# Pair 2's first round by seven products, with the weights' differences made in pairs 0 and 1

## The reference

```
att   = softmax(gelu(gelu(cond @ W0 + b0) @ W1 + b1) @ W2 + b2)      # 64 x 8
agg_w = einsum('bk,koi->boi', att, weight)                           # 64 matrices of 64 x 64
c     = einsum('boi,bih->boh', agg_w, x) + (att @ bias_k)[:, :, None]
out   = c @ W.T + b                                                  # W is 1024 x 1024
lora  = c @ A[:r].T @ B[:, :r].T        # r of (8, 16, 32, 64) by the largest gate score of c
x     = x + out + lora
```

## Time and profile before

| | us |
|---|---|
| median of 3 runs | 445.14 (444.48 to 445.39) |
| the profiled execution | 446.35 |
| its span | 444.8 |
| outside the span | 1.55 |
| PE busy | 438.8 (99% of the span) |
| DVE busy | 277.7 (62%) |
| ACT busy | 125.6 (28%) |
| POOL busy | 21.9 (5%) |

### The profile page before, as it was taken

One profiled execution on the slowest core, in us unless ns is written; L12 is line 12 of the kernel. 1 busy time (PEld: TensorE's weight loads), 2 busy tenths in 40 slices (PEclk: granted clock), 3 DMA queues, 4 the chain that ended last, 5 costly groups with the idle time before them and its releaser, 6 DMA issues.

```text
span 444.8 us, 10164 instructions
## 1 busy us (share of the span) xinstructions
PE 438.8 (99%) x3639; PEld 409.9 (92%) x3639; DVE 277.7 (62%) x695; ACT 125.6 (28%) x262; POOL 21.9 (5%) x46
## 2 busy tenths in 40 slices
PE   8999999999999999999999999999999999999996
PEld 6979999998999999999999999999999999999995
DVE  5959959695573747557374755837475483747533
ACT  5654543532230402223040222314022221302210
POOL 3014000010000000000000000000000000000000
PEclk9999999999999999999999999999999999999999
DMA  7985662607144170714408061340806135070303
GB/s 242 325 237 176 161 212 62 229 1 243 48 153 140 30 264 0 238 51 151 138 14 275 0 235 55 142 147 9 280 0 225 64 140 149 12 273 7 96 1 94
DMA packets 24363, 59.17 MB, mean 133 GB/s; under 512 B 7198, under 2 KB 9298, under 8 KB 24276
## 3 DMA queue, kind: packets, MB, share of 16 engines
q1 hardware_dynamic: 24020, 58.71, 41.1%
q10 hardware_dynamic: 320, 0.14, 0.1%
HBM read 40.69 MB, written 18.15 MB: 132 GB/s over the span
## 4 chain that ended last, share of the span: by engine, by line
PE 97%; DMA 1%; SPq 0%; issue 0%; DVEq 0%; ACT 0%; DVE 0%
PE p_p L1054 79%; PE p_o L1076 8%; PE p_o L1113 4%; PE p_o L1114 4%; DMA w_raw<-in_w 1%; PE p_p L1157 1%; PE p_p L1102 1%; PE p_p L1209 0%; DVEq L87 0%; ACT wh L567 0%; SPq L381 0%; SPq L379 0%; SPq L377 0%; SPq L376 0%; PE p_p L1165 0%
## 5 line engine op out<-in xcount | busy, mean ns | idle before, releaser
L1054 PE MATMUL p_p<-wh,xh 128*128 128x274 f32 (+1 forms) x880 | 258.9, 294 | 0.4 <-ACT wh L567 0.4
L1054 PE MATMUL p_p<-wh,xl 128*128 128x274 f32 (+1 forms) x880 | 254.5, 289 | 0.0
L1054 PE MATMUL p_p<-wl,xh 128*128 128x272 f32 (+1 forms) x864 | 250.1, 290 | 0.4 <-issue 0.4
L1054 PEld LDWEIGHTS p_p<-wh,xh 128*128 128x128 f32 x880 | 166.5, 189 | 7.5 <-issue 6.6
L1054 PEld LDWEIGHTS p_p<-wh,xl 128*128 128x128 f32 x880 | 166.5, 189 | 0.1
L1054 PEld LDWEIGHTS p_p<-wl,xh 128*128 128x128 f32 x864 | 163.0, 189 | 0.6 <-issue 0.6
L778 DVE TENSOR_TENSOR xl<-raw,xh 128x512 fp32r<-128x512 f32 x45 | 31.1, 691 | 49.4 <-ACT xh L598 49.0
L612 ACT ACTIVATE z<-p_p 128x272 f32<-128x272 f32 (+1 forms) x44 | 17.6, 399 | 116.7 <-PE p_p L1054 116.7
L800 DVE TENSOR_TENSOR xl<-s_raw,xh 128x512 fp32r<-128x512 f32 x60 | 40.2, 687 | 16.3 <-ACT xh L604 15.8
L831 DVE TENSOR_TENSOR xin<-p_o,xin 128x274 f32<-128x274 f32 (+2 forms) x128 | 46.3, 414 | 2.1 <-PE p_o L1114 1.3
L824 DVE TENSOR_TENSOR z<-p_p,su 128x274 f32<-128x274 f32 (+1 forms) x56 | 24.7, 441 | 31.8 <-PE p_p L1054 31.4
(11 more groups left out here) (123 smaller groups left out, 288.1 us busy)
## 6 DMA issues: line engine op xcount, KB each, us to landing
xin<-in_x SPq DMA_DIRECT2D x32, 512.0 KB, 4.2
raw<-in_xt SPq DMA_DIRECT2D x30, 512.0 KB, 4.1
out<-xin SPq DMA_DIRECT2D x15, 512.0 KB, 3.2
out<-xin SPq DMA_DIRECT2D x30, 256.0 KB, 3.5
w_raw<-in_w SPq DMA_DIRECT2D x8, 274.0 KB, 7.6
w_raw<-in_w SPq DMA_DIRECT2D x8, 272.0 KB, 6.6
g_aggw<-aggw_all SPq DMA_DIRECT2D x8, 128.0 KB, 2.5
aggw<-g_aggw SPq DMA_DIRECT2D x15, 64.0 KB, 3.3
```

Source lines behind the costliest of these rows:

```text
L1054: last = nc.tensor.matmul(o[:, 0:W[r]], a, m, start=start and p == 0, stop=stop and p == 2, skip_group_check=True)
```

## The change

Round 0 of pair 2 becomes sevenfold: `TERMWISE` goes from 2 to 1. Pair 2 then has no A21 parts and no termwise evictions, but a snapshot, sums of products and S1 to S4 in round 0. The differences of round 0's weights move:

- the four `t_sum(0, ...)` (8 DVE instructions) go from pair 2 to pair 0: R11 and R12 ahead of `route(0, 0)`, R22 and R21 behind the low part of `bt`. For this DVE's `column_sums` moves behind all of `w_lo`, and round 1's `t_sum` are spread: R12 behind pair 0's residuals, R22 behind A12's low part, R21 into pair 1;
- `t_hi(0, ...)` on ACT go to pair 1: R22 ahead of the eviction of Z21, R11 behind it, R12 and R21 at the pair's end;
- `t_lo(0, ...)` on DVE: R22 and R11 in pair 1, R12 and R21 in pair 2's round 0.

```
-T_LOWS = ((R22, R12, R21, R11), (R22, R11, R12, R21))
-TERMWISE = 2
+T_LOWS = (R22, R11, R12, R21)
+TERMWISE = 1
...
@@ ACT, step(i, j)
-                    if not two:
-                        snapshot(i, j, 0)
+                    snapshot(i, j, 0)
...
-                if two:
+                if one:
                     t_hi(0, R22)
-                    t_hi(0, R12)
-                if early(i, j, 0):
                     z_evict(i, j, 0, Z21)
-
-                if two:
-                    t_hi(0, R21)
+                    t_hi(0, R11)
                 snapshot(i, j, 1)
                 if not last:
                     a_hi(i, j + 1, A11)
-                if two:
-                    t_hi(0, R11)
                 z_evict(i, j, 1, Z11)
                 if not last:
                     a_hi(i, j + 1, A12)
                 u_transposed(i, j)
+                if one:
+                    t_hi(0, R12)
+                    t_hi(0, R21)
...
@@ DVE, pair 0
-            w_lo(12)
+            for m in range(12, 16):
+                w_lo(m)
             column_sums()
-            for m in range(13, 16):
-                w_lo(m)
+            t_sum(0, R11, R12, R11)
+            t_sum(0, R12, R22, R12)
             route(0, 0)
             ...
+            dve.wait_ge(s_tsum[0], 4)
+            t_sum(0, R22, R22, R11)
+            dve.wait_ge(s_tsum[0], 6)
+            t_sum(0, R21, R21, R22)
             dve.wait_ge(s_wl, 16)
             t_sum(1, R11, R12, R11)
-            t_sum(1, R12, R22, R12)
-            dve.wait_ge(s_tsum[1], 4)
-            t_sum(1, R22, R22, R11)
             a_lo(0, 1, A11)
             for n in (Z11, Z22, Z12, Z21):
                 residual(0, 0, 0, n)
+            t_sum(1, R12, R22, R12)
             a_lo(0, 1, A12)
-            dve.wait_ge(s_tsum[1], 6)
-            t_sum(1, R21, R21, R22)
+            dve.wait_ge(s_tsum[1], 4)
+            t_sum(1, R22, R22, R11)
...
@@ DVE, step(i, j)
                 if one:
+                    dve.wait_ge(s_tsum[1], 6)
+                    t_sum(1, R21, R21, R22)
...
                     s_lo(i, j, S4)
-                elif two:
-                    (four t_sum(0, ...), s_lo S3 and S4 between them)
                     t_lo(0, R22)
-                    t_lo(0, R12)
                 else:
+                    if two:
+                        t_lo(0, R12)
                     add(i, j, 0, SU2)
                     s_lo(i, j, S3)
+                    if two:
+                        t_lo(0, R21)
                     s_lo(i, j, S4)
...
                 add(i, j, 1, SU2)
-                if two:
-                    t_lo(0, R21)
+                if one:
                     t_lo(0, R11)
```

More of the change, by code:

```diff
@@ L686, in step @@
                 one = is_pair(i, j, 1)
-                two = is_pair(i, j, TERMWISE)
                 if one:
@@ L765, in t_lo @@
                     ks = slice(2 * h, 2 * h + 2)
-                    dve.wait_ge(s_th[r], 2 * T_LOWS[r].index(n) + h + 1)
+                    dve.wait_ge(s_th[r], 2 * T_LOWS.index(n) + h + 1)
                     nc.vector.tensor_tensor(wl[r][:, T_OF[n], ks, :], w_raw[r][:, n, ks, :],
@@ L970, in step @@
                 one = is_pair(i, j, 1)
-                two = is_pair(i, j, TERMWISE)
+                two = is_pair(i, j, TERMWISE + 1)
                 if not one:
@@ L1290, in low_difference @@
                     if first:
-                        pe.wait_ge(s_tl[r], 2 * T_LOWS[r].index(n) + 2)
+                        pe.wait_ge(s_tl[r], 2 * T_LOWS.index(n) + 2)
                 def end(done):
```

## The result

The changed kernel takes 443.29 us in the median of 22 runs. The kernel before, run beside it, takes 445.37 us (22 runs). The ratio is 0.9956, with a 95% interval of 0.994 to 0.9971: 2.0 us less, 1.3 to 2.7. Forecast were 443.0 us and 2.18 us less. One of the 22 runs took 1187.17 us at a full granted clock, for which nothing here gives a cause: it is left out of the ratio, and without it the median is 443.19 us. The kernel was run twice more beside the experiments and had ratios of 0.9967 (0.9948 to 0.9986) and 0.9932 (0.9906 to 0.9957).

A forecast was written before the change was run, and what follows sets the result against it. PE was taken to bound the kernel, busy 438.8 of 444.8 us. Fewer matmuls (1.52) and a closed gap (0.66) sum to 2.18 us off the 445.14 median, giving 443.0 us, range 442.4 to 443.9.

The forecast's parts named there:

- both terms: On PE: 1.52 us from 12 fewer matmuls and 0.66 us from a closed gap; chance of both 0.66.
- 12 matmuls fewer, 1.52 us: Pair 2's round 0 on PE falls from 96 to 84 matmuls, with its step from 13.20 to 11.68 us.
- The gap, 0.66 us, from a late S21: PE's gap ahead of pair 3's mix, blamed on DVE's late S21 sum in pair 2, goes: 0.66 us.
- The moved sums hide in two holes of pair 0: DVE's four added sums fill idle ahead of column sums and route; route on time, A12's slack 0.45 us, cost 0.
- ACT's added roundings don't reach PE: In pair 1 two roundings delay Z21's eviction by 0.62 us; tightest slack to PE 0.18 us, cost 0.
- The slacks: Time to PE's deadlines: A12 in pair 0 0.45 us, Z21 in pair 1 0.18, SV in pair 2 0.5.
- SV in pair 2, 0.45 late: DVE's added low parts in pair 2's round 0 make SV 0.45 us late; slack 0.5, cost 0.
- Rival three: DVE's sums hold up POOL's first `ubias` in pair 0 by 3.40 us: slower, 446.0 us; chance 0.04, partial forms 0.05.
- The profiled execution at 444.2: The profiled execution falls from 446.35 to 444.2 us by 2.18 us, the 1.55 outside its span unchanged.

The follow-up runs named there:

- the run with the gap closed: The kernel before, with low parts R11 and R21 of round 0's weights moved from pair 2's round 1 to pair 3; ratio 1.0006 to the kernel before.
- five dummies: The changed kernel plus five DVE subtractions on scratch data ahead of A12's low part in pair 2's round 1; ratio 0.9998 to the kernel before.
- three dummies: The changed kernel plus three DVE subtractions on scratch data ahead of A12's low part in pair 2's round 1; ratio 0.9966 to the kernel before.
- the run with eight sums: The changed kernel with all eight sums of round 0's weights on DVE ahead of pair 0's route; ratio 0.9954 to the kernel before.

## Why the prediction was right

It was right in its total and in both terms. Device time bears out the total; the two terms, and that nothing was lost beside them, are read from the traces.

- *12 matmuls fewer, 1.52 us*: 13.20 to 11.68 us in the chain, and 27.52 to 26.00 us from the run with the gap closed to the changed kernel.
- *The gap, 0.66 us, from a late S21*: inferred from 101.01 and 101.11, two times on two engines, where the profile named no releaser. Three runs bear it out: take the DVE work away, and it closes; put 3.9 us in, and it comes back with 1.5; put 2.45 in, and 0.07 come.
- *The moved sums hide in two holes of pair 0*: yes. The route is not late, and A12 has 0.56 us (0.45 forecast) to PE's matmul.
- *ACT's added roundings don't reach PE*: yes, 0.31 us left (0.18 forecast). I had counted the eviction 0.62 late; it was 0.52 (58.42 against 58.72, with 0.82 us between the two starts). The idle in brackets, 0.49, was not all that could be filled.
- *The slacks* were all counted to the start of PE's matmul, and that is too late. S21 ended 0.47 us behind that place in the kernel before (101.01 against 100.54) and cost 0.66; with five dummies it was 1.32 behind and cost 1.52; Z21 was 0.78 behind and cost 0.93; with three dummies S21 was 0.11 ahead and cost 0.07. So 0.15 to 0.2 us have to be taken off each slack. By this measure Z21's forecast slack of 0.18 leaves nearly nothing, and the 0.31 that it had leave some 0.15.
- *SV in pair 2, 0.45 late*: it began 4.84 us after the chain's row, against 4.68 in pair 4, so 0.16 late. Too pessimistic, without consequence.
- *Rival three*: refuted for the first `ubias`, see above. In the changed kernel's own profile it didn't even arise, since the four sums end at 30.66 and `ubias` begins at 31.03. For the rule of the Trainium skill ("SBUF — State Buffer", "Who interferes with whom"), that a two-input instruction of DVE and a reading one of GpSimd block each other by the instruction, the run with eight sums agrees: 0.83 us in place of 0.47 amid eight sums, 0.36 more, where one sum is 0.64. What it does not account for is the second `ubias`: when it began (33.47), 0.98 us of `bt`'s low part were left, and it took 1.49 us more than the first in the changed kernel, and 3.40 more in the kernel before.
- *The profiled execution at 444.2*: it was 443.05. The other 1.1 us are the start, which varied by as much as 0.8 us between the three profiles of the changed kernel, and 0.3 us at the end.

## What to carry to other kernels

Where one engine is the chain, compare equal stages in the chain's rows: a stage that is 0.66 us longer with the same work showed a wait to which no releaser was given, and that wait was a third of the gain. For every piece of work moved beside such an engine, count the idle ahead of it and the slack at the deadline, and end the slack 0.15 to 0.2 us ahead of the start that waits for it: within them the work was free, beyond them each run paid it one to one. Against a spread of some microseconds between executions, distances inside one trace settle what five rounds of timing did not.

## What the runs showed of the hardware

POOL's second `ubias`, beside DVE's low part of `bt` and the first sums behind it, took 3.88, 3.88 and 3.24 us in three profiles that have the kernel before's order of sums, and 1.96 or 1.97 in nine with the changed kernel's order and in the one with all eight sums ahead. The changed kernel's:

```profile
31.03 0.47 POOL L541 TENSOR_TENSOR ubias<-bias,gbias 128x136 f32<-128x136 f32 x1
...
33.47 1.96 POOL L541 TENSOR_TENSOR ubias<-bias,gbias 128x136 f32<-128x136 f32 x1 [1.48 <-DVE usplit L847]
```

DVE's six sums took 4.40 to 4.42 us in both orders, so what POOL lost was not DVE's gain. Why POOL loses twice the time in one order stays open. The shape of the sums isn't enough: in the run with all eight ahead the two sums right behind `bt`'s low part were those of the kernel before (128x548), and `ubias` took 1.96.

A store of 2 x 4 KB to DRAM, issued behind 1 MB of loads, was complete after 5.9 to 7.9 us in the nine profiles that have it (29.33 to 36.41 in the changed kernel's, 31.13 to 39.02 with five dummies). Issued ahead of them at 24.35, it was complete by 29.20, under 4.9 us later, and the load did not wait.

A matmul that had waited for a result of DVE or ACT started 0.05 to 0.14 us behind its end (with five dummies SV at 95.94 and 96.08, S22 at 97.68 and 97.73, S21 at 101.55 and 101.65; with R12 ahead of Z21, Z21 at 59.53 and 59.59).
